# Mixture-of-experts network of layer 1: the second routing done by batches, gates multiplied into the output weights, one addition per bank

## What is computed

```python
def _mole(x, W, b, A, Bm, Rw):                 # E, R = 3, 8; SCALING = 1 / R
    gates = jax.nn.softmax(jnp.einsum('bsd,de->bse', x, Rw), axis=-1)
    base = jnp.einsum('bsd,dh->bsh', x, W) + b
    z = jnp.einsum('bsd,edr->ebsr', x, A)
    zg = z * jnp.transpose(gates, (2, 0, 1))[..., None]
    lora = jnp.einsum('ebsr,erh->bsh', zg, Bm)
    return base + SCALING * lora
h = _mole(x, W1, b1, A1, B1, R1)               # 128 -> 512
h = jax.nn.relu(h)
return _mole(h, W2, b2, A2, B2, R2)            # 512 -> 128
...
x = x + gb * _L1_ffn_ref(h, ...)               # gb: one row of 128 gates for each of the 2 batches
h = _layernorm(x, axis=-1) * (1 + ca) + sa     # the layernorm ahead of layer 2
```

## Time and profile before

| | |
|---|---|
| median of 3 runs | 3103.57 us (3103.21 to 3103.8) |
| the profiled execution | 3102.38 us, of which 3100.6 us are its span |
| TensorE (PE) busy in the span | 2855.8 us, 92% |
| VectorE (DVE) busy | 2278.4 us, 73% |
| ScalarE (ACT) busy | 2009.4 us, 65% |
| GpSimd (POOL) busy | 1247.7 us, 40% |
| the mixture network's stage | from 527.97 us to 611.45 us of the span |

### The profile page before, as it was taken

How to read it: one execution, slowest core, us unless ns; L and a number is a source line. 1 busy time by engine, 2 the same in 40 slices (tenths; PEclk the granted TensorE clock), 3 DMA queues, 4 the chain that set the end, 5 groups by cost and what they waited for, 6 DMA issues and landing times.

```text
span 3100.6 us, 88177 instructions
## 1 busy us (share of the span) xinstructions
PE 2855.8 (92%) x36340; PEld 1712.8 (55%) x36340; DVE 2278.4 (73%) x3900; ACT 2009.4 (65%) x5732; POOL 1247.7 (40%) x968
## 2 busy tenths in 40 slices
PE   5789898878898999997799999999999999999997
PEld 3644577523444233333476666666666666666664
DVE  4830595299504777775798888888888888888885
ACT  5541664374313566665688888778888788887885
POOL 0110011000002111111577766766776676677662
PEclk7589855889998999998899999999999999999999
DMA  2000100000002100001232333233232333322221
GB/s 109 3 1 0 39 4 2 1 0 0 0 0 83 53 24 20 24 24 41 60 77 59 79 70 98 73 70 103 57 82 68 96 77 70 101 59 68 68 62 49
DMA packets 48240, 153.41 MB, mean 49 GB/s; under 512 B 11552, under 2 KB 13856, under 8 KB 45952
## 3 DMA queue, kind: packets, MB, share of 16 engines
q1 hardware_dynamic: 47584, 144.41, 17.9%
q10 hardware_dynamic: 288, 3.76, 0.3%
HBM read 43.60 MB, written 5.44 MB: 16 GB/s over the span
## 4 chain that ended last, share of the span: by engine, by line
PE 57%; issue 19%; DVE 11%; ACT 7%; POOL 2%; DVEq 1%; POOLq 1%; ACTq 1%; DMA 0%; SPq 0%
PE ps L1725 14%; PE ps L1743 5%; PE ps L1778 5%; DVE arena L1189 4%; PE ps L1787 4%; PE ps L1800 4%; PE ps L1285 4%; PE ps L1313 4%; PE ps L1760 3%; PE ps L1300 3%; PE ps L1769 3%; PE ps L1806 2%; DVE arena L2193 1%; PE ps L1752 1%; ACT arena L2077 1%
## 5 line engine op out<-in xcount | busy, mean ns | idle before, releaser
L1725 PE MATMUL ps<-arena 128*128 128x512 f32 x1152 | 563.1, 611 | 12.4 <-ACTq L2012 11.9
L2077 ACT ACTIVATE arena<-ps,arena 128x64 f32<-128x64 f32 x1536 | 460.2, 320 | 86.1 <-DVE arena L2273 81.8
L2350 POOL TENSOR_TENSOR arena<-arena 128x1024 f32<-128x1024 f32 x190 | 447.7, 2362 | 98.9 <-DVE arena L2162 98.9
L2356 POOL TENSOR_TENSOR arena<-arena 128x2048 f32<-128x2048 f32 x95 | 344.5, 3626 | 224.7 <-ACT arena L2019 219.1
L1463 DVE TENSOR_REDUCE arena<-ps 128x1 f32<-128x512 f32 x512 | 329.2, 686 | 77.7 <-PE ps L1285 72.6
L1424 ACT ACTIVATE arena<-ps 128x1024 f32<-128x1024 f32 x256 | 262.5, 1025 | 166.4 <-PE ps L1300 166.0
L2077 ACT ACTIVATION_READ_ACCUMULATOR arena<-ps,arena 128x1 f32 x1536 | 324.4, 211 | 0.0
L1725 PEld LDWEIGHTS ps<-arena 128*128 128x128 f32 x1152 | 197.2, 191 | 177.5 <-issue 152.9
L2157 DVE TENSOR_TENSOR arena<-ps,arena 128x1024 f32<-128x1024 f32 x192 | 234.1, 1219 | 42.3 <-PE ps L1725 42.2
L200 POOL TENSOR_SCALAR rstd<-mv 128x4 f32<-128x4 f32 x32 | 7.3, 228 | 636.5 <-DVE mv L186 635.3
L2162 DVE TENSOR_TENSOR arena<-ps,arena 128x512 f32<-128x512 f32 x384 | 245.3, 679 | 0.0
(11 more groups left out here) (295 smaller groups left out, 5564.0 us busy)
## 6 DMA issues: line engine op xcount, KB each, us to landing
arena<-pack_l SPq DMA_DIRECT2D x144, 256.0 KB
arena<-grow SPq DMA_DIRECT2D x144, 256.0 KB
arena<-in_deep SPq DMA_DIRECT2D x5, 2649.5 KB, 10.7
arena<-pack_l SPq DMA_DIRECT2D x96, 128.0 KB
arena<-grow SPq DMA_DIRECT2D x84, 128.0 KB
pack_tern<-in_tern SPq DMA_DIRECT2D x2, 2888.0 KB, 10.3
arena<-in_rotary SPq DMA_DIRECT2D x5, 1024.0 KB, 7.5
arena<-scr_q SPq DMA_DIRECT2D x96, 48.0 KB
```

Source lines behind the costliest of these rows:

```text
L1725: last = T.matmul(m.ps[0:rows.stop - rows.start, at + half, :], f.xs[t % 2][:, rows], w.wqkv[:, j * INNER + half * BLK:j * INNER + (half + ...
L2077: last = A(f.prob[:, p, :], m.ps[:, 4 + j % 2, i * SPAN:(i + 1) * SPAN], ACT.Exp, bias=f.nmax[t % 2][:, p:p + 1], accum_out=f.rsum[t % 2][ ...
L2350: G.tensor_tensor(f.rot[t % 2][:, here], f.rot[t % 2][:, here], f.sin[:, here], ALU.add)
L2356: G.tensor_tensor(r, r, spread(f.ss[t % 2], DH), ALU.mult).then_inc(s["rotated"], 1)
```

## The change

Four things, all in the mixture network.

- Right after the first routing VectorE multiplies both batches' rows of gates into copies of the output weights: `w2g` (128 of the 155 columns; the 27 routing columns are copied as they are) and `b2g`. TensorE uses these copies in the second product and the second low-rank product.
- The second routing is done by batches: batch 0's after bank 2, while TensorE is at banks 3 to 5; batch 1's after bank 5. After bank 5 TensorE turns batch 0's two blocks, adds batch 0's three outputs, and only then turns batch 1's blocks.
- ScalarE does the exponential of batch 0 after the last relu, then the copy of turned block 0, then the exponential of batch 1, then the other copies.
- VectorE's two instructions per bank (multiply, add) are one addition of PSUM and x.

```diff
@@ mole_tensor
-    for bank in range(6):
-        ...  T.matmul(..., f.a[:, k, t * P:(t + 1) * P], f.w2[:, k, :], ...)
-    pe.wait_ge(s["gated"], 2)
-    for i in range(NBLK):
-        if i >= 2:
-            pe.wait_ge(s["zT"], NBLK + i - 1)
-        ...  T.transpose(m.ps[:, 6 + i % 2, t * P:(t + 1) * P], f.zg[:, 4 * i + t, :], m.ident)
-    for bank in range(6):
-        ...  T.matmul(..., f.zT[:, t * P:(t + 1) * P], f.b2, ...)
+    def seconds(bank):
+        ...  T.matmul(..., f.a[:, k, t * P:(t + 1) * P], f.w2g[:, bank // 3, k, :], ...)
+    def turns(b):
+        pe.wait_ge(s["gated"], 3 + b)
+        if b == 0:
+            pe.wait_ge(s["hidden"], NBLK * HB)
+        for i in (2 * b, 2 * b + 1):
+            if b == 1:
+                pe.wait_ge(s["zT"], NBLK + i - 1)
+            ...  T.transpose(m.ps[:, 6 + i % 2, t * P:(t + 1) * P], f.zg[:, 4 * i + t, :], m.ident)
+    def outputs(b):
+        for bank in range(3 * b, 3 * b + 3):
+            pe.wait_ge(s["zT"], NBLK + tiles[-1] // 4 + 1)
+            ...  T.matmul(..., f.zT[:, t * P:(t + 1) * P], f.b2g[:, b, :], ...)
+    pe.wait_ge(s["gated"], 2)
+    for bank in range(6):
+        seconds(bank)
+    turns(0)
+    outputs(0)
+    turns(1)
+    outputs(1)
@@ mole_scalar, after the 16 relus
+    exponentials(slice(0, BT), 2)
+    turned(0, 6, NBLK + 1)
+    exponentials(slice(BT, TILES), 3)
+    for i in range(1, NBLK):
+        turned(i, 6 + i % 2, NBLK + i + 1)
@@ mole_vector
+    def gated_outputs():
+        for b in range(BATCH):
+            gate = gate_row(m, 1, FFN, b)
+            V.tensor_tensor(f.w2g[:, b, :, 0:P], f.w2[:, :, 0:P], repeat(gate, HB), ALU.mult)
+            V.tensor_copy(f.w2g[:, b, :, P:WIDE2], f.w2[:, :, P:WIDE2])
+            last = V.tensor_tensor(f.b2g[:, b, :], f.b2, gate, ALU.mult)
+        last.then_inc(s["gated"], 1)
+    def seconds(b):
+        ...  # the copies of banks 3 * b to 3 * b + 2
+        routed(slice(BT * b, BT * (b + 1)), 2 + b)
+    def added(b):
+        for bank in range(3 * b, 3 * b + 3):
+            ...
+            V.tensor_tensor(x, wide[:, :, 0:P], x, ALU.add)
+            if bank % 3:
+                ln_block(nc, dve, m, ln, 4, 2 * b + bank % 3 - 1)
+    routed(slice(0, TILES), 1)
+    gated_outputs()
+    seconds(0)
+    seconds(1)
+    added(0)
+    added(1)
-        add_gated(nc, dve, m, wide[:, :, 0:P], tiles[0], n, repeat(gate_row(m, 1, FFN, bank // 3), n), ...)
```

More of the change, by code:

```diff
@@ L940, in mole_tensor @@
             for k in range(HB):
-                last = T.matmul(m.ps[:, bank, at:at + WIDE2], f.a[:, k, t * P:(t + 1) * P], f.w2[:, k, :],
+                last = T.matmul(m.ps[:, bank, at:at + WIDE2], f.a[:, k, t * P:(t + 1) * P], f.w2g[:, bank // 3, k, :],
                                 start=t == tiles[0] and k == 0, stop=k == HB - 1, skip_group_check=True)
         last.then_inc(s["low"], 1)
-    pe.wait_ge(s["gated"], 2)
-    for i in range(NBLK):
-        if i >= 2:
-            pe.wait_ge(s["zT"], NBLK + i - 1)
-        for t in range(4):
-            last = T.transpose(m.ps[:, 6 + i % 2, t * P:(t + 1) * P], f.zg[:, 4 * i + t, :], m.ident)
-        last.then_inc(s["turned"], 1)
@@ new lines, in turns @@
+    def turns(b):
[5 more added lines that the diff above has]
+                pe.wait_ge(s["zT"], NBLK + i - 1)
+            for t in range(4):
+                last = T.transpose(m.ps[:, 6 + i % 2, t * P:(t + 1) * P], f.zg[:, 4 * i + t, :], m.ident)
+            last.then_inc(s["turned"], 1)
+    def outputs(b):
+        for bank in range(3 * b, 3 * b + 3):
+            tiles = mole_tiles(bank)
+            pe.wait_ge(s["zT"], NBLK + tiles[-1] // 4 + 1)
+            for t in tiles:
+                at = mole_bank(t)[1]
+                last = T.matmul(m.ps[:, bank, at:at + P], f.zT[:, t * P:(t + 1) * P], f.b2g[:, b, :], start=False,
+                                stop=True, skip_group_check=True)
+            last.then_inc(s["y"], 1)
@@ new lines, in mole_tensor, with mole_scalar, exponentials, turned @@
+    pe.wait_ge(s["gated"], 2)
+    for bank in range(6):
[4 more added lines that the diff above has]
+    outputs(1)
+def mole_scalar(nc, act, m, s, f):
+    def exponentials(tiles, step):
+        act.wait_ge(s["logits"], step)
+        nc.scalar.activation(f.lg[:, tiles, :], f.lg[:, tiles, :], ACT.Exp).then_inc(s["exped"], 1)
+    def turned(i, bank, done):
+        act.wait_ge(s["turned"], done)
+        nc.scalar.activation(f.zT[:, i * BLK:(i + 1) * BLK], m.ps[:, bank, :], ACT.Copy).then_inc(s["zT"], 1)
+    exponentials(slice(0, TILES), 1)
+    for i in range(NBLK):
+        turned(i, 1 + i, i + 1)
+    for n in range(NBLK * HB):
+        i, j = divmod(n, HB)
+        act.wait_ge(s["hid"], n + 1)
+        nc.scalar.activation(f.a[:, j, i * BLK:(i + 1) * BLK], m.ps[:, n % 8, :], ACT.Relu).then_inc(s["hidden"], 1)
+    exponentials(slice(0, BT), 2)
[3 more added lines that the diff above has]
+        turned(i, 6 + i % 2, NBLK + i + 1)
@@ L1042, in mole_setup @@
     f.zT = a.take(TOK)
-    f.tmp = a.take(2 * BLK).rearrange("p (a b) -> p a b", a=2)
+    f.w2g = a.take(BATCH * HB * WIDE2).rearrange("p (c a b) -> p c a b", c=BATCH, a=HB)
+    f.b2g = a.take(BATCH * P).rearrange("p (c b) -> p c b", c=BATCH)
     return f
```

56 lines of the change are left out of this document (25 added, 31 removed).

## The result

| | before | changed |
|---|---|---|
| median of the runs | 3103.53 us (10 runs) | 3095.12 us (10 runs, 3092.41 to 3098.80) |
| ratio, with its 95% interval | | 0.9968 (0.9960 to 0.9975) |
| profiled execution, its span | 3102.38, 3100.6 us | 3092.41, 3090.6 us |
| tail of the mixture stage, in the profiles | 587.53 to 611.45: 23.9 us | 585.54 to 602.13: 16.6 us |

The kernel became faster, as forecast, and by more than forecast. 3095.12 us lies 1.4 us under the 3096.5 predicted, and inside the range of 3094.0 to 3100.0. But the forecast was 7.1 us less, and here the medians differ by 8.4 us, the means by 8.9, and the ratio says 9.9 (7.8 to 12.4). By the ratio, the 3103.57 us that the prediction started from become 3093.6, just under the range.

What follows compares the result with a forecast made beforehand. The part to gain was 24 us of hops between engines after the second product; 4.35 + 1.27 + 1.62 - 0.1 = 7.1 us off 3102.38 gives 3095.3, plus 1.2 for the median: 3096.5 us, range 3094.0 to 3100.0.

Steps and rivals of the forecast that it cites:

- Gated weights and the arena cost nothing: Six extra VectorE instructions, 2.7 us, hide in VectorE's idle time; TensorE streaming weights from the arena costs nothing.
- Batch 0's routing fits in ahead of bank 3's copy: Second routing: batch 0's takes 2.6 us from 579.06, gates out at 581.7, bank 3's copy at 582.2.
- First addition 2.9 us after bank 5's copy, 4.35 us gained: VectorE's first addition starts at 590.5 instead of 594.88, waiting for its own routing and no longer for TensorE.
- The exponential's wait behind the copy: On ScalarE, batch 1's exponential stands behind the copy of turned block 0, a new wait of 0.3 us.
- Additions 1.27 us: VectorE, one addition per bank instead of two instructions: two banks take 1.03 and not 2.30 us.
- GpSimd 1.62 us, at 2.15 us a block with roots of 1.04: Layernorm after the additions: GpSimd works back to back, four blocks in 7.86 instead of 9.48 us.
- ScalarE 0.1 us lost: Layernorm: normalization plus modulation take 2.35 us a block against GpSimd's 2.15, charged at 0.1 us.
- The clock does not fall behind the last bank: Forecast against the rival that TensorE drops to 1.2 GHz after bank 5, cutting the gain to 4.6 us; rival's chance 0.1.
- The sum, 7.1 us: Total gain in the mixture stage's tail: 4.35 + 1.27 + 1.62 - 0.1 us.
- The tail up to 611.45 is otherwise the same: The remaining work up to the next stage's first matmul was taken as unchanged, adding no term to the sum.
- The next stage starts in a worse moment for the clock: Rival: one low-clock stretch behind the stage added (3098.1 us, chance 0.15) or removed (3094.9 us, chance 0.07).

Runs made afterwards that it cites:

- the kernels that were filled behind the stage: Changed kernel and kernel before, each with constant matmuls in TensorE's waits of the layernorm behind the mixture stage: medians 3093.74 and 3100.76 us.
- the gap with a low stretch of 4.3 us: Changed kernel plus VectorE memsets of a dead buffer at the mixture stage's end, delaying the next stage by 2.6 us: ratio 0.9980 to kernel before.

## Where the prediction was right, and the step that failed

- *Gated weights and the arena cost nothing.* Right. The six extra instructions took 1.9 us (from 536.31 to 538.25), where 2.7 were estimated, under the turning of the first routing, and the second product took 17.12 us against 17.10.
- *Batch 0's routing fits in ahead of bank 3's copy.* Right: 2.5 us, forecast 2.6.
- *First addition 2.9 us after bank 5's copy, 4.35 us gained.* Right: 2.94 us in the changed kernel, 4.4 us of tail in the version with batches alone. The exponential's wait behind the copy was real; putting it first gave 0.15 us, where the prediction had put the wait at 0.3.
- *Additions 1.27 us.* Right: two banks took 1.01 and not 2.30.
- *GpSimd 1.62 us, at 2.15 us a block with roots of 1.04.* Right in its size: four blocks took from 591.05 to 598.91, 7.86 us. The version with gated weights alone gained 2.65 us of tail for both terms, forecast 2.9. The reason given for 1.04 was partly misread. The addition in the earlier trace rows covers 0.69 us of that root and not all of it, and in the changed kernel no root runs beside an addition at all, only beside statistics. The rule of the Trainium skill, "GPSIMD Engine Reference", "Key points", that two SBUF inputs contend with GpSimd, agrees with the roots of the kernel before (1.17, 1.36 and 1.24 us beside an addition with both inputs in SBUF, 1.04 beside none); no run tests it apart from the number of additions.
- *ScalarE 0.1 us lost.* It did not come: from GpSimd's end to the next stage are 3.23 us before and 3.22 after.
- *The clock does not fall behind the last bank.* Right: it stays at 1.00 for 9.1 us. Here transposes at full level, 8 in 1.03 us, stand between matmuls.
- *The sum, 7.1 us.* Right for the profile that it was made against (7.3: 4.41 + 1.29 + 1.62), and in agreement with the kernels that were filled behind the stage (6.9, give or take 1.3). Too small for the kernels as they are: 8.9 and 9.7 us in the means, with standard errors of 0.8 and 0.9.

The step that failed is the baseline: "The tail up to 611.45 is otherwise the same", and with it the assumption that the one profile stood for the kernel before, so that the sum has no term for TensorE's clock. In that profile the clock had been low for 3.4 us under the transposes, and for 3.1 at the start of the next stage. In the four others it was low for 6.8 us under the transposes in three, and for 4.8 to 6.1 at that start in all. The mean of five profiles is 24.4 us of tail and 183.1 of state-space stage; the three of the changed kernel have 16.6, and 182.2 in the mean. These two terms give 7.8 + 0.9 = 8.7 us where the prediction had 7.1 + 0. Layers 2 and 3 give another 1.1 in the profiles (666.0 against 664.9), but in the filled pair they stand the other way round (666.3 for the changed kernel, 665.0 for the other), so I do not count this as the change's doing.

The mechanism stood in the prediction as a rival, "The next stage starts in a worse moment for the clock", with 0.15 for a loss and 0.07 for a gain of this kind (3094.9 us). The gain is what came. I had given it little because I did not ask how the kernel before itself stood to this risk: it had an idle TensorE of 3 us ahead of the transposes, after which the clock fell in all five profiles, and the change removes the place.

How far this is shown: the tail's part (7.8 us in the mean and not 7.3) is read from five profiles against three. That a start at the full level shortens the state-space stage is shown too, 180.5 us in both filled kernels. That the low start of the kernel before is what makes the rest of the excess is inferred. It fits the filled pair, but with an error of 1.3 us. Two things do not fit it: the version with the exponential first had the long state-space stage, 183.5 us, without losing in its total, and the gap with a low stretch of 4.3 us did not lengthen it. Nor is it shown how often each alignment occurs among the runs that were not profiled. Open as well is what decides between a low stretch of 2.8 and one of 6.3 us at the start of the state-space stage: the version with the exponential first began it only 0.15 us sooner after bank 5's copy, at 602.0, and stayed at the low level until 608.3.

## What to carry to other kernels

A sum made against one profile inherits where that execution's clock falls happened to land; if a stage to be changed has an idle TensorE of about 3 us in it or behind it, take several profiles of the kernel before and compare stage lengths before trusting the terms to 1 us. A change that fills or removes such an idle stretch can gain, beside the work that it hides, the low stretches that followed on it. And when two engines overlap in a chain, ask what one does to the other: here each root of GpSimd was 0.1 to 0.3 us longer while VectorE added out of two buffers in SBUF, and was not with that instruction gone.

## What the runs showed of the hardware that I had not expected

- Identical code ahead of the change took 525.6 to 531.4 us in eight profiles, and the clock's changes stood differently in them; the state-space stage took 182.1 to 183.5 us for the same instructions, and 180.5 where TensorE started it at the full level.
- The clock rose after a stretch with nothing but transposes in it. In the changed kernel's first routing 16 of them ran from 536.45 to 540.12 us at 0.50, behind an idle TensorE of 3.47 us, and the clock was at 1.00 from 540.2 on.
- The last 60 us of the program hold longer falls of the clock in some executions than in others: the last stage took 1629.2 us in four profiles and 1626.3 in most, and between them in four more. One kernel can have both, since the kernel before took 1626.3 to 1626.4 four times and 1628.6 once. So it is not shown that the edits some 2400 us ahead decide it.
- VectorE paused 0.38 us, waiting for nothing that the profile shows, ahead of each 128x2048 memset, and 0.39 us ahead of batch 1's L1032, but not ahead of batch 0's. In the version with the batches alone that pause is gone from there, and one of 0.43 us stands a few instructions later, ahead of the first L268.
